# A two-layer graph network on one core: sixteen block slots, a ring of five for block combinations, and 84 instead of 89 blocks multiplied by seven products

## What is computed

```python
h = relu(layernorm(x)); x = x + adj @ (h * (u >= 0.1) / 0.9)   # layer 1
h = relu(layernorm(x)); x = x + adj @ (h @ W) + b              # layer 2
```

## Time and profile before

| | us |
|---|---|
| median of three runs | 905.43 (900.5 to 907.24) |
| the profiled execution | 905.17 |
| its span | 903.4 |
| TensorE busy | 869.5 |
| VectorE busy | 581.1 |
| moved by the transfers | 363.72 MB, 403 GB/s in the mean |

### The profile page before, as it was taken

One profiled execution on the slowest core, in us unless ns is written; L12 is line 12 of the kernel. 1 busy time (PEld: TensorE's weight loads), 2 busy tenths in 40 slices (PEclk: granted clock), 3 DMA queues, 4 the chain that ended last, 5 costly groups with the idle time before them and its releaser, 6 DMA issues.

```text
span 903.4 us, 13460 instructions
## 1 busy us (share of the span) xinstructions
PE 869.5 (96%) x5556; PEld 486.4 (54%) x5556; DVE 581.1 (64%) x1234; ACT 42.7 (5%) x120; POOL 2.6 (0%) x13
## 2 busy tenths in 40 slices
PE   6799999999989999999999999999989999999998
PEld 5445444444444544667576755645546556568543
DVE  5364633323354567686788877888768887898824
ACT  3100000000000000000000000000000000000000
POOL 1000000000000000000000000000000000000000
PEclk9999999999999999999999999999999999999999
DMA  9999999999999999999999999999999999999995
GB/s 375 420 420 419 422 422 420 421 420 416 422 420 421 420 420 400 423 420 420 391 421 384 422 368 389 412 367 394 403 374 362 410 392 398 415 420 420 416 421 202
DMA packets 52636, 363.72 MB, mean 403 GB/s; under 512 B 5696, under 2 KB 5984, under 8 KB 10208
## 3 DMA queue, kind: packets, MB, share of 16 engines
q1 hardware_dynamic: 52512, 362.83, 98.4%
q0 software_dynamic: 64, 0.03, 0.0%
HBM read 360.74 MB, written 2.10 MB: 402 GB/s over the span
## 4 chain that ended last, share of the span: by engine, by line
PE 79%; DMA 17%; DVE 2%; SPq 2%; issue 1%; DVEq 0%
PE banks L824 27%; PE banks L849 22%; DMA blocks<-in_adj 17%; PE row_sums L799 15%; PE row_sums L855 5%; PE banks L818 5%; PE banks L834 3%; SPq L518 1%; PE banks L951 0%; DVE quarters L680 0%; PE banks L918 0%; DVE blocks L678 0%; DVE quarters L676 0%; PE row_sums L918 0%; PE row_sums L808 0%
## 5 line engine op out<-in xcount | busy, mean ns | idle before, releaser
L824 PE MATMUL banks<-blocks,features 128*64 128x512 f32 x1200 | 362.8, 599 | 6.4 <-DMA blocks<-in_adj 6.3
L799 PE MATMUL row_sums<-blocks,features 128*64 128x512 f32 x984 | 241.1, 593 | 9.2 <-DMA blocks<-in_adj 9.1
L824 PEld LDWEIGHTS banks<-blocks,features 128*64 128x64 f32 x1200 | 120.2, 138 | 138.5 <-issue 134.8
L849 PE MATMUL banks<-quarters,mixed 128*64 128x256 f32 x712 | 168.5, 379 | 0.1
L714 DVE TENSOR_TENSOR acc<-acc,banks 128x512 f32<-128x512 f32 (+1 forms) x101 | 69.1, 685 | 140.1 <-PE banks L824 116.4
L799 PEld LDWEIGHTS row_sums<-blocks,features 128*64 128x64 f32 x984 | 91.4, 137 | 118.2 <-issue 99.5
L849 PEld LDWEIGHTS banks<-quarters,mixed 128*64 128x64 f32 x712 | 97.4, 137 | 32.4 <-DVE quarters L682 0.8
L818 PE MATMUL banks<-blocks,features 128*64 128x512 f32 x224 | 98.1, 592 | 0.1
L849 PE MATMUL banks<-quarters,features 128*64 128x256 f32 x356 | 91.5, 379 | 0.0
L855 PE MATMUL row_sums<-blocks,mixed 128*64 128x256 f32 x356 | 91.4, 379 | 0.0
L849 PE MATMUL banks<-blocks,features 128*64 128x256 f32 x356 | 91.4, 379 | 0.0
(11 more groups left out here) (65 smaller groups left out, 594.5 us busy)
## 6 DMA issues: line engine op xcount, KB each, us to landing
blocks<-in_adj SPq DMA_DIRECT2D x339, 1024.0 KB, 10.8
x<-in_x SPq DMA_DIRECT2D x2, 1024.0 KB, 7.7
acc<-in_u SPq DMA_DIRECT2D x2, 1024.0 KB, 9.9
out<-x SPq DMA_DIRECT2D x7, 256.0 KB, 3.2
blocks<-in_adj SPq DMA_DIRECT2D x2, 512.0 KB, 25.8
out<-x SPq DMA_DIRECT2D x2, 128.0 KB, 1.8
w_twice<-in_wb POOLq DMA_DIRECT2D x2, 16.2 KB, 6.0
```

The lines of the kernel that those rows point to most:

```text
L799: return nc.tensor.matmul(row_sums[at, t.unit % 2, nodes], features[:, tile_of(k, j), 0:D], tile, start=start, stop=last and t.n == unit_l ...
L824: return nc.tensor.matmul(banks[at, t.sum.bank, nodes], features[:, tile_of(t.k, j), D:2 * D], tile, start=t.n == t.sum.first and j == t.t ...
L849: return nc.tensor.matmul(banks[half * D:(half + 1) * D, SUM_BANKS + bank, nodes_of(column)], by[:, j, :], of[:, j, :], start=opens and fi ...
```

## The change

- `SLOTS` is 16 instead of 15. 8 KB of each partition more for `blocks` come from the buffers below.
- `quarters` is a ring of five combinations instead of two sets of three. A seven's third combination lies where the first of the seven before lay, so it is made on its own, in `make_last_quarter`, at the turn `t.at_last`: not before the previous seven, and behind a wait until TensorE has ended that one.
- `turned` is now the first half of set 0 of `mixed`, and `centring`, `square` and `dev` are parts of set 1. The centred row is written over the turned row, and the squares go to the row's bank of PSUM. Two waits go with that: VectorE waits for `h2_ready` of its own unit before it writes `mixed`, and TensorE, before the first matmul of unit m, for `h2_ready` of unit m - 2 and no longer only for its turned row.
- From row 13 on, s - 12 of the blocks of row s that were sevens are items "both", spread over the row by k. These are (13,12), (14,6), (14,13), (15,4) and (15,9). The places of all 335 items stay as they are. Nothing differs before item 268, (13,12).

```diff
 KEPT = 2
-SLOTS = 15
+SLOTS = 16
...
 SEVEN_FROM = 4
-SEVEN_LOAD, SEVEN_MADE, SEVEN_SETS = 2, 3, 2
+SEVEN_LOAD, SEVEN_MADE, SEVEN_SETS, QUARTERS, SEVENS = 2, 3, 2, 5, 12
...
@@ -140,7 +142,8 @@
     def both(self, s, k):
-        whole = s < SEVEN_FROM or (s, k) == (BLOCKS - 1, BLOCKS - 2)
+        spread = k * max(0, s - SEVENS) // s != (k + 1) * max(0, s - SEVENS) // s
+        whole = s < SEVEN_FROM or spread or (s, k) == (BLOCKS - 1, BLOCKS - 2)
         return Item("both" if whole else "seven", [self.operand(s, k)], k, s, s + 1)
...
@@ -278,7 +281,8 @@
     for n, t in enumerate(sevens):
         t.nth, t.set = n, n % SEVEN_SETS
         t.at = max(t.n - SEVEN_MADE, t.loads()[0].released, sevens[n - SEVEN_SETS].n if n >= SEVEN_SETS else 0)
-        assert t.at < t.n
+        t.at_last = max(t.at, sevens[n - 1].n if n else 0)
+        assert t.at_last < t.n
...
-        centring = sb("centring", [P, 2 * D])
         w_twice = sb("w_twice", [P, D + 1])
...
-        quarters = sb("quarters", [P, SEVEN_SETS, 3, TILES // 2, HALF_BLK])
+        quarters = sb("quarters", [P, QUARTERS, TILES // 2, HALF_BLK])
         mixed = sb("mixed", [P, SEVEN_SETS, 4, TILES // 2, D])
-        square = sb("square", [P, N // P])
-        dev = sb("dev", [P, N // P])
         total2 = sb("total2", [P, TILES])
         square2 = sb("square2", [P, TILES])
         dev2 = sb("dev2", [P, TILES])
-        turned = sb("turned", [P, TILES, D])
-        centred2 = sb("centred2", [P, TILES, D])
-        squares2 = sb("squares2", [P, TILES, D])
+        turned = mixed[:, 0, 0:2, :, :].rearrange("p n t d -> p (n t) d")
+        centring = mixed[:, 1, 0, :, :].rearrange("p t d -> p (t d)")
+        square, dev = mixed[:, 1, 1, 0, :], mixed[:, 1, 1, 1, :]
...
+        def combined(t, n):
+            return quarters[:, (3 * t.nth + n) % QUARTERS, :, :]
...
@@ -622,7 +631,8 @@
                 shape = [P, tiles, D]
                 mine, sums_of_row = turned[:, 0:tiles, :], x1_of(m)
                 mean, var, std = total2[:, 0:tiles], square2[:, 0:tiles], dev2[:, 0:tiles]
-                centre, power = centred2[:, 0:tiles, :], squares2[:, 0:tiles, :]
+                power = row_sums[:, m % 2, 0:tiles * D].rearrange("p (t d) -> p t d", d=D)
                 dve.wait_ge(used, max(unit_last[m].values()) + 1)
...
                 link2(nc.vector.tensor_reduce(mean, mine, AX.X, ALU.add))
-                link2(nc.vector.scalar_tensor_tensor(out=centre, in0=mean.unsqueeze(2).to_broadcast(shape),
+                link2(nc.vector.scalar_tensor_tensor(out=mine, in0=mean.unsqueeze(2).to_broadcast(shape),
                                                      scalar=-1.0 / D, in1=mine, op0=ALU.mult, op1=ALU.add))
-                link2(nc.vector.tensor_tensor(power, centre, centre, ALU.mult))
+                link2(nc.vector.tensor_tensor(power, mine, mine, ALU.mult))
                 nc.vector.tensor_reduce(var, power, AX.X, ALU.add).then_inc(h2_summed, 1)
                 dve.wait_ge(h2_dev, m + 1)
                 link2(nc.vector.reciprocal(var, std))
                 nc.vector.scalar_tensor_tensor(
-                    out=features[:, unit_tiles(m), D:2 * D], in0=centre, scalar=0.0,
+                    out=features[:, unit_tiles(m), D:2 * D], in0=mine, scalar=0.0,
                     in1=var.unsqueeze(2).to_broadcast(shape), op0=ALU.max, op1=ALU.mult)\
                     .then_inc(h2_ready, 1)
...
                 b11, b12, b21, b22 = (features_of(t, tiles, layer) for tiles in range(2) for layer in (1, 2))
                 t1, t2, t3, t4 = (mixed[:, t.set, n, :, :] for n in range(4))
-                dve.wait_ge(h2_ready, t.needs)
+                dve.wait_ge(h2_ready, t.unit)
                 if t.nth >= SEVEN_SETS:
                     dve.wait_ge(used, sevens[t.nth - SEVEN_SETS].n + 1)
                 nc.vector.tensor_tensor(t1, b12, b11, ALU.subtract).then_inc(seven_mixed, 1)
@@ -671,15 +682,19 @@
                 nc.vector.tensor_tensor(t2, b22, t1, ALU.subtract).then_inc(seven_mixed, 1)
                 dve.wait_ge(seven_mixed, 4 * t.nth + 3)
                 nc.vector.tensor_tensor(t4, b21, t2, ALU.subtract).then_inc(seven_mixed, 1)
-                s1, s2, s4 = (quarters[:, t.set, n, :, :] for n in range(3))
                 dve.wait_ge(block_arrived[t.loads()[0].slot], t.loads()[0].arrived)
-                nc.vector.tensor_tensor(s1, a21, a22, ALU.add).then_inc(seven_made, 1)
+                nc.vector.tensor_tensor(combined(t, 0), a21, a22, ALU.add).then_inc(seven_made, 1)
                 nc.vector.tensor_tensor(a21, a11, a21, ALU.subtract).then_inc(seven_made, 1)
                 dve.wait_ge(seven_made, 4 * t.nth + 1)
-                nc.vector.tensor_tensor(s2, s1, a11, ALU.subtract).then_inc(seven_made, 1)
+                nc.vector.tensor_tensor(combined(t, 1), combined(t, 0), a11, ALU.subtract).then_inc(seven_made, 1)
+            def make_last_quarter(t):
+                if t.nth:
+                    dve.wait_ge(used, sevens[t.nth - 1].n + 1)
                 dve.wait_ge(seven_made, 4 * t.nth + 3)
-                nc.vector.tensor_tensor(s4, a12, s2, ALU.subtract).then_inc(seven_made, 1)
+                nc.vector.tensor_tensor(combined(t, 2), quarter(t, 0, 1), combined(t, 1), ALU.subtract)\
+                    .then_inc(seven_made, 1)
...
@@ -757,6 +772,8 @@
                 for t in sevens:
                     if t.at == n:
                         make_quarters(t)
+                    if t.at_last == n:
+                        make_last_quarter(t)
                 if n - 1 in unit_end:
...
                 a11, a12, s3, a22 = (quarter(t, nodes, tiles) for nodes in range(2) for tiles in range(2))
-                s1, s2, s4 = (quarters[:, t.set, n, :, :] for n in range(3))
+                s1, s2, s4 = (combined(t, n) for n in range(3))
                 b11, b12, b21, b22 = (features_of(t, tiles, layer) for tiles in range(2) for layer in (1, 2))
                 t1, t2, t3, t4 = (mixed[:, t.set, n, :, :] for n in range(4))
...
             def multiply(t):
                 s, m = t.row, t.unit
                 if m is not None and m >= 2 and t.n == min(unit_first[m].values()):
-                    pe.wait_ge(row_placed, (m - 1) * (P // SQ))
-                    pe.wait_ge(row_placed_act, (m - 1) * (P // SQ))
+                    pe.wait_ge(h2_ready, m - 1)
                 if s == 0:
                     pe.wait_ge(xd_ready, t.k // 2 + 1)
```

More of the change, by code:

```diff
@@ L293, in plan @@
     unit_end = {max(t.n for t in items if t.unit == m): m for m in range(UNITS)}
+    assert all(t.at >= max(n for n, m in unit_end.items() if m < t.unit) + 2 for t in sevens)
     sums, row_sum = [], {}
```

## The result

| | before | changed |
|---|---|---|
| median of the runs (range) | 906.03 us (900.5 to 907.24, 4 runs) | 894.57 us (893.59 to 895.39, 4 runs) |
| ratio | 1 | 0.9895 [0.9872, 0.9918] |
| profiled execution (span) | 905.17 us (903.4) | 895.39 us (893.6) |

The changed kernel is 1.05% faster. Profiled execution against profiled execution it is -9.8 us, where -9.65 was predicted. With the repetition further down, ten runs of the changed kernel have a median of 895.28.

What follows compares the result with a forecast made beforehand. It took the transfer queue to bound before 430 us, late slot releases to 735 and TensorE after. Slot -10.9, whole blocks +2.05 - 0.8, ring and rest 0 sum to -9.65: 905.17 becomes 895.5 us, range 890.0 to 902.0.

Steps and rivals of the forecast that it cites:

- What bounds: Whole kernel: the transfer queue limits before 430 us, late slot releases from 430 to 735 us, where 13.8 us hang on them.
- The slot, -10.9 us: Sixteenth slot, rows 9 to 14: shorter block waits and no half clock give 12.4 us, less 1.5 set against them.
- the 2.5 at most that I asked for: Sign of being right: the array's waits for blocks between 430 and 735 us total 2.5 us or less.
- Each row gains anew: Rows 9 to 14: slots fill again between drains, so each drain's wait shrinks by at most 2.49 us.
- the 1.5 us: Set against the slot's 12.4 us: blocks landing unevenly, a gap of 0.5 to 1 us late in a drain becoming a wait.
- The half clock, -3.8 us: Items behind the two longest waits: both half-clock stretches go, as no wait over 1.0 us is left; 3.8 us saved.
- Whole blocks, +2.05 - 0.8: Five blocks whole instead of by seven: +2.05 us of TensorE, less 0.8 of row 15 waits for VectorE; net +1.25 us.
- The ring of five, 0 with +2 as the bound: A seven's last combination, waiting for the seven before: slack of about 1.2 us suffices, cost 0, upper bound +2 us.
- the VectorE rival: 37 back-to-back sevens: the last combination comes too late, 25.5 us if each waits, giving 921.0 us; chance 0.06.
- Squares in PSUM, 0: 17 squares written to PSUM and read back on VectorE: no difference by the rows, 0 us.
- The transfer rival: Dip from 430 to 735 us: the transfers' own rate sets it, not slots, so 906.4 us; chance 0.16.
- The half clock rival: Waits shrink, but some other wait lets the clock fall twice: 899.3 us; chance 0.18.

Runs made afterwards that it cites:

- extra_early: s15_k84 plus six loads of one block into a spare buffer that nothing reads, all before 360 us: 918.9 us, ratio 1.0164 to the kernel before.
- extra_gap: s15_k84 plus four loads into an unread spare buffer, ahead of loads 205, 229, 256 and 280: 911.99 us, ratio 1.009 to the kernel before.
- after_again: The changed kernel once more, with no edit: 896.46 us over 6 runs, ratio 0.9913 to the kernel before.
- s16_k89: The changed kernel with all 89 blocks by seven instead of 84, still 16 slots: 896.57 us, ratio 0.9936 to the kernel before.
- s15_k84: The changed kernel with 15 slots instead of 16, all else as changed: 904.62 us, ratio 1.0019 to the kernel before.
- s15_k89: The changed kernel with 15 slots and all 89 blocks by seven: 905.14 us, ratio 1.0035 to the kernel before.
- s15_k89_ring6: The changed kernel with 15 slots, 89 sevens and a ring of six without the wait for the seven before: 903.15 us, ratio 0.9986 to the kernel before.
- the three sets: The groups in which the experiments, edits of the changed kernel, ran, each beside the kernel before: its medians 903.35, 904.54 and 904.14 us.
- s16_k86: The changed kernel with 87 sevens (despite the label) instead of 84, row 15 ending with six in a row: 895.08 us, ratio 0.9905 to the kernel before.
- s16_bal95: The changed kernel with the planner letting loads fill 0.95 of a row's time instead of 0.97: 894.78 us, ratio 0.9906 to the kernel before.

## Why the prediction was right, point by point

- **What bounds.** Right. The queue bounds before 430 us (`extra_early`: 14.3 of 14.9 us). After it the slots do: one fewer takes the gain back. The prediction saw them as late releases alone. The table under `extra_gap` adds how: with fewer slots fewer loads are on their way, and the rate is lower.
- **The slot, -10.9 us.** Right. It measured -10.1 (-9.3 against all ten runs, -9.6 to -11.2 by the ratios) at 84 sevens and -8.6 at 89, and 11.3 between the two profiled executions. Inside it two terms were off and partly cancel. The waits left are 3.3 us, not the 1.2 or so of the sum nor the 2.5 at most that I asked for: 3.49 us became 1.24, close to the 1.0 reckoned, but 2.33 became 1.70 where I let it go whole. The 1.24 is on the lucky side: the same wait is 2.31 us in `after_again` and 2.53 in `s16_k89`, also with 16 slots. From the end of the first item to the end of the second wait only 0.2 us was gained, 0.6 with the 0.41 of (13,12), which lies between. So the second drain did not get the full block that the first did: the array came to it 8.9 us earlier, and its last load had one more ahead of it. "Each row gains anew" was too simple. This is the loss for which the 1.5 us stood.
- **The half clock, -3.8 us.** It went in the first profile. The size was 1.7 + 1.7 = 3.4 us: I had compared a length that counts the last matmul's end (5.35) with one that doesn't (3.43). From start to start it is 5.15 against 3.46 and 3.44. The reason that I gave, that no wait over 1.0 us is left, is not what happened: 1.24 and 1.70 are left. And the waits alone don't decide it, since 3.19 and 2.73 us in `s15_k84` were followed by full clock and 2.31 us in `after_again` by half. So that both stretches went in this execution is in part luck. Over many runs the clock is higher: the ten runs of the changed kernel have a mean granted clock of 0.997, the 51 of the kernel before in the three sets 0.994.
- **Whole blocks, +2.05 - 0.8.** The 0.41 us each was right. The rest was mis-sized. The changed kernel's chain shows both lengths, 3.02 us for the seven (15,3) from 791.97, and 6.87 for two whole blocks from 794.99, (15,4) and (15,14), which is 3.43 each:

```profile
791.97 0.16 PE banks L866
...
794.99 0.38 PE row_sums L816
...
801.86 0.16 PE banks L866
```

  But the five blocks buy back 1.8 us of waits for L696 (2.3 to 0.5), not 0.8, by which the net would be +0.25. Measured, it was -0.5 us at 15 slots and -1.3 to -2.0 at 16 instead of +1.25. Each median is uncertain by 1 to 2 us, so this is nothing or a small gain.
- **The ring of five, 0 with +2 as the bound.** This step failed. It costs 1.5 us of waits at 89 sevens (`s15_k89` against `s15_k89_ring6`), and 2.0 us between their medians, 4.4 by the ratios, each of which is uncertain by about 2 us. I had worked out a slack of 1.2 us for one pair of sevens and 0.5 us more loss for those behind it, and then took 0. VectorE's idle time before L696 in the changed kernel (busy, mean ns, idle before, and for what) shows how long the new wait holds it:

```profile
L696 DVE TENSOR_TENSOR quarters<-blocks,quarters 128x512 f32<-128x512 f32 x84 | 58.2, 692 | 53.7 <-PE banks L866 47.9
```

  47.9 us of waiting for the seven before, in 27 of the 84, and the array loses nothing by it that its waits show. The 0.5 us that it does lose, in row 10, has another reason: the last combination now stands behind an add. The rows after, on VectorE and then TensorE:

```profile
494.20 0.68 DVE L729 TENSOR_TENSOR acc<-acc,banks 128x512 f32<-128x512 f32 x1
494.80 0.69 DVE L696 TENSOR_TENSOR quarters<-blocks,quarters 128x512 f32<-128x512 f32 x1
...
495.54 0.43 PE L866 MATMUL banks<-quarters,mixed 128*64 128x256 f32 x1
```

  L696 starts right behind the add, with no wait of its own, ends at 495.49, and the matmul that needs it starts at 495.54. In the kernel before the combination at this place (495.12) comes ahead of the add (495.73). The prediction named an add queued ahead only as a condition of the VectorE rival and left its 0.68 us out of the slack. In row 15 the slack is used up by length: three waits at the end of seven sevens (`s16_k89`), two at the end of six (`s16_k86`), none in the changed kernel, whose longest run there is four.
- **These two errors have opposite signs.** The net of ring and whole blocks is +1.25 in the sum. By the medians it is 904.62 - 903.35 = +1.3 at 15 slots. So the sum came out by terms that were each wrong by about 2 us, and that it came within 0.2 us of the profiled -9.8 is luck.
- **Squares in PSUM, 0.** Right. The write takes 417 ns against 409, the reading 409 against 404: 17 x 13 ns = 0.2 us on VectorE, hidden.

```profile
L661 DVE TENSOR_TENSOR row_sums<-mixed 128x256 f32<-128x256 f32 (+1 forms) x17 | 7.1, 417 | 0.6
L662 DVE TENSOR_REDUCE square<-row_sums 128x4 f32<-128x256 f32 (+1 forms) x17 | 6.9, 409 | 0.6
```

  By the Trainium skill ("VectorE: DVE Perf Modes", TRN2 errata) the reading would have been 65 ns longer, an estimate from that page. The row shows 5, and the measurement decides.
- **Rivals.** The transfer rival (906.4) fell with `s15_k84`. The half clock rival (899.3) fell in the first profile, where rows 13 and 14 run at full clock. The profiled execution of `after_again`, 898.17 us, has one half clock in row 13 again. So it is less frequent now, not gone: four of the ten runs have that execution's mean granted clock, 0.996, the others 0.998 or more. The VectorE rival (921.0) fell as stated, each of 37 sevens late: there is one wait, of 0.5 us. `s16_bal95` shows where it would begin.

## What to carry to other kernels

Price one more buffer drain by drain: find the drains whose transfer starts at a release, take for each the smaller of its wait and one transfer, and add what the wait itself brings in half clock. Count the loads on their way as well: a buffer that is not free is a transfer not begun. Do not count a second drain in full if the first one's gain moves the array closer to the queue. When a resource is paid for by a tighter ring, date the new wait over the longest run of such items, not over one pair, since the loss of each adds to the next, and add what the new place in the order puts ahead of it.

## What the runs showed of the hardware

- **The same wait brings half clock in one execution and not in another.** In row 4 both kernels wait alike. Before, the eight records behind it take 1.94 us, after, 3.63:

```profile
254.81 1.94 PE L799 MATMUL row_sums<-blocks,features 128*64 128x512 f32 x8 [3.03 <-DMA blocks<-in_adj]
```
```profile
254.98 3.63 PE L816 MATMUL row_sums<-blocks,features 128*64 128x512 f32 x8 [3.04 <-DMA blocks<-in_adj]
```

  A wait of 2.33 us was followed by half clock in the earlier trace rows, waits of 2.73 and 3.19 us in `s15_k84` by full clock (the items take 3.65 us). The length of the last wait alone does not tell.
- **The spread from run to run goes with this clock.** Of the 51 executions of the kernel before in the three sets, the 17 with a mean granted clock of 0.996 or more have a median of 901.05 us, the 13 with 0.992 or less 905.5. Longer waits may be behind both. The changed kernel's ten runs spread over 4.6 us (893.59 to 898.17), those of before, which are more, over some 9.
- **A buffer short costs more than the last one gained.** 14, 15 and 16 slots take 932.5, 904.62 and 894.57 us. Beyond the waits, the granted clock falls to 0.97 with 14.
- **With few loads on their way the transfers move less.** In the kernel before, from 430 to 735 us, it is 383 GB/s with at most three 1 MB loads on their way and 405 with four or more. Up to 430 us, where four or more are on their way for 93% of the time, it is 419.
